# Rounding of the input rows moved from the start into the first steps of the loop, in an attention and mixture-of-experts block on one NeuronCore

## The reference, cut to what matters

```python
y = clip(ln(layernorm(x)) / in_scale, -448, 448)      # one in_scale vector for each of k, v, q, qx
xq = y.astype(bfloat16).astype(float8_e4m3fn)         # rounding to 8 bits
k, v, q, qx = (linear(xq_of_its_own, w) for each)     # 8 groups of heads
core = softmax(ln(q) ln(k)^T) v                       # self-attention
xout = softmax(ln(qx) ln(kx)^T) vx                    # attention over the context rows
```

## Time and profile before

| | |
|---|---|
| median of 3 runs | 824.04 us (821.97 to 824.12) |
| the profiled execution, its own time | 820.62 us |
| its span in the trace | 818.8 us |
| PE, DVE busy over the span | 724.2 us (88%), 607.0 us (74%) |
| ACT, POOL busy over the span | 464.3 us (57%), 455.8 us (56%) |

### The profile page before, as it was taken

How to read it: one execution, slowest core, us unless ns; L and a number is a source line. 1 busy time by engine, 2 the same in 40 slices (tenths; PEclk the granted TensorE clock), 3 DMA queues, 4 the chain that set the end, 5 groups by cost and what they waited for, 6 DMA issues and landing times.

```text
span 818.8 us, 15329 instructions
## 1 busy us (share of the span) xinstructions
PE 724.2 (88%) x4859; PEld 586.4 (72%) x4859; DVE 607.0 (74%) x1290; ACT 464.3 (57%) x1178; POOL 455.8 (56%) x592
## 2 busy tenths in 40 slices
PE   3548999899999989999998999999976786999996
PEld 2536877788878777887877887887754554777775
DVE  6856888787888878888887888887887692444554
ACT  3646767667676766767666776766743231222221
POOL 3464767666667756676765667676655313222220
PEclk9869999999999999999999999999999796999999
DMA  5310000100000010000001010000020103666661
GB/s 181 107 54 26 1 27 1 49 30 27 27 1 27 1 53 26 26 27 2 27 1 52 2 33 27 1 2 0 1 59 1 38 28 109 192 186 189 198 193 53
DMA packets 44479, 42.74 MB, mean 52 GB/s; under 512 B 3718, under 2 KB 43387, under 8 KB 44411
## 3 DMA queue, kind: packets, MB, share of 16 engines
q1 hardware_dynamic: 42874, 36.62, 14.8%
q0 software_dynamic: 1536, 5.28, 2.4%
HBM read 39.52 MB, written 2.37 MB: 51 GB/s over the span
## 4 chain that ended last, share of the span: by engine, by line
PE 50%; DVE 19%; ACT 12%; issue 9%; POOL 7%; SPq 2%; DMA 1%; DVEq 0%; ACTq 0%; POOLq 0%
PE out_ps L1717 8%; PE aux_ps L1534 8%; PE proj_ps L1442 5%; ACT p_sb L792 5%; DVE q_tok L1083 4%; PE aux_ps L1471 4%; PE pT_ps L1510 4%; PE proj_ps L1433 4%; PE work_ps L1709 3%; POOL y_bf L548 3%; POOL catq L551 3%; PE work_ps L1731 2%; PE s_ps L1501 2%; ACT y_bf L806 2%; PE proj_ps L1457 2%
## 5 line engine op out<-in xcount | busy, mean ns | idle before, releaser
L541 POOL TENSOR_SCALAR p_sb<-p_sb,psum_row 128x256 f32<-128x256 f32 x256 | 121.1, 488 | 78.9 <-DVE psum_row L1102 78.8
L792 ACT ACTIVATE p_sb<-s_ps,negmax 128x256 f32<-128x256 f32 x256 | 118.0, 474 | 33.5 <-DVE negmax L1097 32.7
L1108 DVE COPY pT_sb<-pT_ps 128x512 f32<-128x512 f32 x128 | 87.7, 686 | 52.0 <-PE pT_ps L1510 50.9
L1520 PE MATMUL aux_ps<-pT_sb,v_sb 128*128 128x512 f32 x256 | 121.2, 595 | 3.5 <-DVE pT_sb L1108 3.5
L548 POOL TENSOR_TENSOR y_bf<-y_bf,mg_bf 128x512 bf16<-128x512 bf16 x64 | 86.1, 1345 | 63.8 <-DVE mg_bf L1120 63.8
L1501 PE MATMUL s_ps<-kT,qT 128*128 128x256 f32 x768 | 115.1, 292 | 6.0 <-DVE qT L1093 3.8
L1501 PEld LDWEIGHTS s_ps<-kT,qT 128*128 128x128 f32 x768 | 97.8, 190 | 15.9 <-issue 15.9
L526 POOL TENSOR_TENSOR rstd<-var,minus_half 128x8 f32<-128x8 f32 (+1 forms) x64 | 86.6, 1352 | 5.5 <-POOL var L522 0.4
L1097 DVE TENSOR_REDUCE negmax<-s_ps 128x2 f32<-128x512 f32 x128 | 86.2, 680 | 4.1 <-PE s_ps L1501 4.1
L1534 PE MATMUL aux_ps<-wpT,catq 128*128 128x256 f32 x512 | 70.9, 293 | 17.7 <-POOL catq L551 15.0
L806 ACT ACTIVATE y_bf<-aux_ps,rvec 128x256 bf16<-128x256 f32 x128 | 53.9, 478 | 51.0 <-PE aux_ps L1520 51.0
(11 more groups left out here) (174 smaller groups left out, 1366.6 us busy)
## 6 DMA issues: line engine op xcount, KB each, us to landing
w_up_a<-in_L_ffn_gate_up_proj SPq DMA_DIRECT2D x16, 384.0 KB, 3.6
w_up_b<-in_L_ffn_gate_up_proj SPq DMA_DIRECT2D x16, 384.0 KB, 3.6
wp_raw<-in_L_xattn_wproj SPq DMA_DIRECT2D x16, 256.0 KB, 2.9
w_down_a<-in_L_ffn_down_proj SPq DMA_DIRECT2D x16, 192.0 KB, 3.6
w_down_b<-in_L_ffn_down_proj SPq DMA_DIRECT2D x16, 192.0 KB, 3.6
w_raw<-in_L_xattn_w_kv_x SPq DMA_DIRECT2D x8, 256.0 KB, 3.9
w_raw<-in_L_xattn_wq SPq DMA_DIRECT2D x7, 256.0 KB, 2.7
w_raw<-in_L_xattn_wqx SPq DMA_DIRECT2D x7, 256.0 KB, 3.0
```

Of the source, the lines that this page charges most:

```text
L541: ins = nc.gpsimd.tensor_scalar(p_sb[:, r, st, :], p_sb[:, r, st, :], rsum[:, r, st:st + 1], 1.0, ALU.mult, ALU.mult)
L792: ins = nc.scalar.activation(p_sb[:, r, st, :], s_ps[:, r % 2, st, :], ACT.Exp, bias=negmax[:, r, st:st + 1], accum_out=psum_row[:, r, st: ...
L1108: nc.vector.tensor_copy(pT_sb[:, r // 2, r % 2, :, :], pT_ps[:, r % 2, :, :]).then_inc(pT_ready, 1)
L1520: ins = nc.tensor.matmul(aux_ps[:, f.bank, :], v_sb[:, (2 * s.n + tt) % VRING, ty, s.gi, :], pT_sb[:, ty, :, tt, :], start=(tt == 0), stop ...
```

## The change

It does five things. (1) The first batch is rounded in halves: the copies for k and v first (`X_TYPES` sets the order), all of it on DVE with the final subtraction too (L1015 of the changed kernel), ahead of `weight_scales`; the copies for q and qx later. (2) The second key projection, (0, 1), moves from step 0 to right behind the first and writes to the banks of `pT_ps`; its sums and reciprocal roots have places of their own. (3) Batch 1 is rounded in step 0, batch 2 in step 1, batch 3 in step 3, each in two halves on DVE and POOL, through buffers over expert weights (`w_up_a`, `w_down_a`) that are loaded later now. (4) The projection (1, 0) moves from the head of step 1 to behind the first two scores. (5) The eight scalars are loaded by ACT's queue instead of SP's.

```diff
+        q_y0 = as_bf16(wp_raw[:, :, :, :].rearrange("p a b c -> p (a b c)"))
+        q_mg0 = as_bf16(qk_f[:, :, :].rearrange("p a b -> p (a b)"))
+        q_y1 = as_bf16(w_down_a[:, :, :, :].rearrange("p a b c -> p (a b c)"))
+        q_mg1 = as_bf16(w_up_a[:, :, :, :, :].rearrange("p u e c j -> p (u e c j)")[:, 0:4 * H])
...
+        X_TYPES = (1, 2, 0, 3)
+        def kv_ps(n, t):
+            return pT_ps[:, :, :, :].rearrange("p a b c -> p a (b c)") if (n, t) == (0, 1) else proj_ps[:, :, :]
...
 sync engine
-            for i, name in enumerate(SCALARS):
-                sp.dma_start(scal[:, i:i + 1], t[name].partition_broadcast(P)).then_inc(scal_loaded, 16)
...
-            sp.wait_ge(aux_filled, Fill("WQ", 1, 0).filled)
-            for u in range(2):
-                load_pair(u, u)
+                if j == 0:
+                    sp.wait_ge(xq_ready, 2 * NB - 1)
+                    for u in range(2):
+                        load_pair(u, u)
...
 gpsimd
             for count in range(7):
                 ln_rstd(count)
-            quant_sub(0)
             ln_rstd(7)
+            quant_sub(0, 1)
...
             rstd_kv(0, 0)
-            quant_sub(1)
+            rstd_kv(0, 1)
...
-                if kv:
+                if kv and i > 1:
                     rstd_kv(*kv)
-                if i == 0:
-                    quant_sub(2)
                 if s1:
                     p_norm(s1, 0)
                     p_norm(s1, 1)
+                if i == 1:
+                    rstd_kv(*kv)
...
                 if i == 0:
-                    quant_sub(3)
+                    quant_sub(1, 0)
+                    quant_sub(1, 1)
                 if s1:
                     p_norm(s1, 2)
                     p_norm(s1, 3)
+                if i in (1, 3):
+                    quant_sub(2 + i // 2, 0)
+                    quant_sub(2 + i // 2, 1)
...
 scalar engine, step i
                 if s1:
                     exps(s1, 2)
                     exps(s1, 3)
+                if i in (1, 3):
+                    quant_y(2 + i // 2)
+                if s1:
                     y_of(s1, 0)
...
 vector engine
-            def quant(b):
+            def quant(b, half):
...
+                if (b, half) == (0, 0):
+                    link(nc.vector.tensor_tensor(y, y, mg, ALU.add))
+                    nc.vector.tensor_tensor(xq[:, 0, 0:2, :, :].rearrange("p a c k -> p (a c) k"), y, mg, ALU.subtract
+                                            ).then_inc(xq_kv_ready, 1)
+                else:
+                    nc.vector.tensor_tensor(y, y, mg, ALU.add).then_inc(z_ready, 1)
...
+            quant(0, 0)
             weight_scales()
-            quant(0)
             ctx_lo(0)
...
             ctx_lo(2)
             ctx_lo(3)
+            quant(0, 1)
             for step in LN_STEPS[12:]:
                 ln_step(*step)
...
                 if s0:
                     scaled_q(s0)
+                if i == 0:
+                    quant(1, 1)
+                if i in (1, 3):
+                    quant(2 + i // 2, 0)
                 if s1:
                     recip(s1, 3)
                     evac_pT(s1, 2)
+                if i in (1, 3):
+                    quant(2 + i // 2, 1)
+                if s1:
                     magic(s1, 0)
...
 tensor engine
             project_kv(0, 0)
+            project_kv(0, 1)
+            fill_wq(0, 0)
+            fill_wq(1, 0)
             transpose_h(2)
             transpose_h(3)
-            fill_wq(0, 0)
-            fill_wq(1, 0)
...
                 if s1:
                     scores(s1, 0)
                     scores(s1, 1)
+                if i == 1:
+                    project_kv(*kv)
```

More of the change, by code:

```diff
@@ L661, in quant_y @@
                 act.wait_ge(yT_ready, b + 1)
-                wait(act, xq_ready, b - 1)
-                for ty in range(4):
+                wait(act, xq_ready, 2 * b - 1 if b > 1 else 0)
+                for t, ty in enumerate(X_TYPES):
                     for c in range(HC):
-                        ins = nc.scalar.activation(q_y[b % 2][:, ty * HC + c, :], yT[:, b, c, :], ACT.Copy,
+                        ins = nc.scalar.activation((q_y1 if b else q_y0)[:, t * HC + c, :], yT[:, b, c, :], ACT.Copy,
                                                    scale=rvec[:, INS + 2 * ty + c:INS + 2 * ty + c + 1])
+                    if t == 1:
+                        ins.then_inc(y_ready, 1)
                 ins.then_inc(y_ready, 1)
@@ L1193, in _ @@
                     recip(s1, 1)
+                if i == 1:
+                    sums(kv_seq(*kv), 4)
+                    scaled_kv(*kv)
                 if s2:
```

121 lines of the change are left out of this document (65 added, 56 removed).

## The result

The kernel after the change takes 833.88 us (median of 4 runs, 833.14 to 835.57), the kernel before 824.08 (median of 4 runs, 821.97 to 824.33). The ratio is 1.0123, with a 95% interval of 1.01 to 1.0146: the change makes the kernel about 10 us slower. The forecast was 831.8, from 818 to 836, with 0.6 on slower.

A forecast was written before the change was run, and what follows sets the result against it. The start has no engine at its limit; a chain of waits, then a ring of steps, bounds it. Start -8.0, roundings +8.1 and +7.7 sum to +7.8 us: 828.4 from profiled 820.62, 831.8 against the median; 8 in 10 between 818 and 836.

The forecast's parts named there:

- The start, "8.0 earlier": From program start to the scaling of sub-step 1: first queries scaled 10.2 us earlier, 2.2 given back, 8.0 earlier.
- I take 0, at most 1: Scalars on ACT's queue share DMA engines with the input rows; delay of the rows taken as 0, at most 1 us.
- PE's second fill, "1.1": In the start, PE's second fill of low parts of the query weights, eight matmuls, taken as 1.1 us.
- the clock stays low: Rival: first query projection and step 1's key projection at half clock take 1.6 and 1.5 more; +10.9, 835 us; chance 0.12.
- The layer norm's tail, held by POOL: 2.0 later: In the start, POOL's 2.1 us subtraction blocks the last two scalings of the layer norm: end at 35.3, 2.0 later.
- The rounding in step 1, "8.1 us later": Batch 2: DVE and POOL take turns, so the scaling of key projection (1, 1) begins 8.1 us later.
- T: Time of the query scaling of sub-step 1, 77.03 us before the change; forecast near 69.
- The rounding in step 3, "7.7 us later": Batch 3, same order as in step 1, but exponentials end 0.35 ahead of the scaling: 0.4 less, 7.7 us later.
- At nothing: Costs taken as zero: later expert weight loads, SP's wait for the last rounding, and the scalars' eight issues on ACT.
- The rival without whole-instruction waits: DVE isn't held for POOL's whole instructions: start -9.5, roundings 4.4 and 4.0 later; sum -1.1, 823 us; chance 0.18.
- The gaps: Rival: rounding slips into POOL's idle 1.62 us ahead of `round_cat`, 2.6 lost each time; -4.3, 819.7 us; chance 0.18.
- PE idle before the query projection of steps 2 and 4: Sign that the forecast is right: PE stands idle there, with the second key scaling 16 to 17 us behind T.

The follow-up runs named there:

- e1: The changed kernel with the eight scalars loaded by SP's queue again, behind the query weights; 832.44 us, single run.
- e6: e5 with scalars on SP's queue, the layer norm's tail behind the query weights, and batch 1's second half rounded later; 824.53 us, single run.
- e9: e6's early start; subtraction of half (1, 0) on DVE, batch 2 rounded mid-step 1, batch 3 in pairs through steps 2 to 5; 816.06 us, single run.
- e11: e9 with POOL's subtraction of (2, 0) waiting for DVE's rounding of (2, 1), whose subtraction goes into step 2; 813.97 us median, ratio 0.9894 to before.
- e2: The changed kernel with batches 2 and 3 left unrounded, zeros written to their rows by POOL in the start; 818.68 us, single run.
- e7: The changed kernel with only POOL's subtractions kept for batches 2 and 3, on old data, without ACT's and DVE's part; 825.78 us, single run.
- e8: The changed kernel without POOL's subtractions for batches 2 and 3, zeros in their place, ACT's and DVE's part kept; 825.42 us, single run.
- e3: The changed kernel with the four subtractions of batches 2 and 3 made by DVE instead of POOL; 835.10 us, single run.
- e4: The changed kernel with batches 2 and 3 rounded behind the step's last DVE and ACT work, subtractions in the next step; 839.12 us, single run.
- e5: The changed kernel with batches 2 and 3 rounded in pieces, one half in each of steps 1 to 4, subtractions a step later; 827.18 us, single run.

## Why the prediction was right, and where its terms were off

The sign and the mechanism held; that the number came so near is in part luck. The sum was +7.8 and the profiles, from which its terms were taken, differ by 12.5: 3.4 more in the start, 0.7 less in the two roundings, 2.0 more behind step 3. Against the medians it is 831.8 forecast and 833.88 measured; this miss is smaller because the profile of before lies further under its median than that of after.

- **The start, "8.0 earlier": 4.6.** This is the term that was mis-sized, by 3.4. "I take 0, at most 1" for the scalars was too little: the rows landed at 5.02, not 3.75, and of that 1.3, 0.9 was left at the end of the layer norm (36.17, forecast 35.3); e1, e6, e9 and e11 confirm the cause by taking it away (they land at 3.50 to 3.60 there, at 4.98 to 5.07 in the eight others). PE's second fill, "1.1", was 1.4 dearer, since it ran at half clock; with 0.24 for the projection and 0.33 less behind it, the first scaling ended 2.2 late (51.51, forecast 49.3). From the turning of the queries to the next projection 13.1 was forecast and 12.9 came: the key projection in series costs what was said. Then that projection took 3.51 for 2.13. So some 2.8 of the 3.4 are the clock, and the rival "the clock stays low" came true in part, with other matmuls than those it named.
- **The layer norm's tail, held by POOL: 2.0 later.** Nearly as forecast: the two scalings took 2.52 in place of 0.73, 1.8 more.
- **The rounding in step 1, "8.1 us later": 7.9.** The order of turns is that of the text but for its ends, and the two held instructions measured 2.22 and 2.10. The key scaling came at T + 16.0, forecast T + 16.6. That it is so near is luck as well. On POOL the chain was 1.2 shorter than forecast, with the key root ending at T + 15.35: one more DVE instruction was through ahead of the first subtraction, and the low part of the queries ran beside `round_cat` (83.44, 83.60), not ahead of it. What the sum had not was the half clock of the scores behind the idle 5.48 us, which kept DVE from the key scaling for 0.67 more.
- **The rounding in step 3, "7.7 us later": 7.2**, at 15.6 behind its query scaling.
- **At nothing.** Behind the loop 1.5 us went to a low clock in the router and the first experts. No term stood for it, and it comes and goes between runs: e1 has the fast rows there, e2 the slow ones. The later weight loads are not the cause: e1 has the loads of after, and e11, whose last rounding and so whose loads come later still, has fast rows too (1.19 and 4.45).
- **The rival without whole-instruction waits** (T + 12.9, 823) is refuted by the held instructions of after and e7, which e8 has short (0.43 and 0.29), and by e3, which takes POOL away: the key scaling moved by 1.1, as the account by turns had it. The Trainium skill, page "SBUF — State Buffer", section "SBUF: two separate sides", has these engines lock a shared pair of ports for a whole instruction, where VectorE runs in a two-port mode or reads two inputs from SBUF; the trace agrees, with 2.22 and 2.10 us, and with the 2.48 in e1 for the low part of the queries, which has two inputs.
- **The gaps** (819.7): refuted for this order, since `recip` stood behind the first half, as the argument against it said; POOL waited 3.06 for it. In another order it is nearly true: e9 loses 1.8 for batch 3, and e11 some 3.2 for both (2.0 behind T, 1.2 ahead of it).
- **"PE idle before the query projection of steps 2 and 4"**: the 5.48 us stand ahead of the scores, one place earlier in the same chain.

What stays open is the clock's share in the start. The same code gave T between 72.4 and 74.1, and no run could hold the clock fixed. That kernels with an earlier first scaling give back part of it by T (e1 all, e6 a quarter) is shown: from the one to the other it is 24.1 in e1 and 23.3 in e6, against 22.0 to 22.5. In e1 the clock is not the only cause, since the held low part of the queries comes first; in e6 that one is not held (0.69), and the scores run at half clock again (2.91). That the clock alone does it is not shown.

## What to carry to other kernels

Price moved work not by its busy time (some 4.2 us on POOL for each rounding, two subtractions of 2.1) but by what stands behind it on its two queues, plus the time for which the engines hold each other; one rounding cost 7.5 us here (after), 10.2 (e4), 5.4 (e5) or at most 2 (batch 3 in e9 and e11), by its place and the pieces that it is cut into. An idle place is free only if the next thing on that engine waits for something still later; ahead of a reciprocal root on POOL nothing is free. Put POOL's long instructions where DVE reads PSUM or reduces, as e11 does, and if a start is won by some microseconds, look whether TensorE's clock, or an instruction that now meets POOL's, gives them back before counting them.
